# First attention of a fused four-stage kernel: scores of two heads on two row halves of TensorE, P divided on GpSimd, transposes late in a step

## What is computed

```python
h = silu(x @ W1.T + b1) @ W2.T + b2
q, k, v = split(h @ Wg.T + bg)              # 16 heads of 64
dots = einsum('bhid,bhjd->bhij', q, k) / 8
dots = where(j >= i + 64, -inf, dots)       # banded from above
attn = softmax(dots)
out  = einsum('bhij,bhjd->bhid', attn, v) @ Wo.T + bo
```

## Time and profile before

| | |
|---|---|
| median of 3 runs | 1743.43 us |
| span of the profiled execution | 1814.1 us |
| TensorE busy | 1434.0 us, 79% of the span |
| VectorE busy | 1064.9 us, 59% |
| ScalarE busy | 973.5 us, 54% |
| GpSimd busy | 448.9 us, 25% |
| first attention | about 34 to 770 us of the span |

### The profile page before, as it was taken

How to read it: one execution, slowest core, us unless ns; L and a number is a source line. 1 busy time by engine, 2 the same in 40 slices (tenths; PEclk the granted TensorE clock), 3 DMA queues, 4 the chain that set the end, 5 groups by cost and what they waited for, 6 DMA issues and landing times.

```text
span 1814.1 us, 32941 instructions
## 1 busy us (share of the span) xinstructions
PE 1434.0 (79%) x8094; PEld 974.1 (54%) x8094; DVE 1064.9 (59%) x3974; ACT 973.5 (54%) x2664; POOL 448.9 (25%) x495
## 2 busy tenths in 40 slices
PE   7999999999999999818999999125676667567581
PEld 4666665666665656416788888112344344335351
DVE  2677777777777777636443343025466556656555
ACT  6777777777777777414455555002344334334454
POOL 1012111222222212125100000665434433441003
PEclk9999999999999999859999999656788778878896
DMA  9000000000000000022122222144334333332301
GB/s 342 1 10 12 12 12 12 12 12 12 12 12 12 10 10 12 11 81 64 59 67 69 64 69 66 38 63 57 49 54 51 50 41 56 49 49 42 41 2 46
DMA packets 76443, 78.90 MB, mean 43 GB/s; under 512 B 10769, under 2 KB 69650, under 8 KB 75954
## 3 DMA queue, kind: packets, MB, share of 16 engines
q1 hardware_dynamic: 55378, 49.77, 13.9%
q0 software_dynamic: 8192, 16.79, 3.3%
q10 hardware_dynamic: 12816, 11.67, 1.9%
HBM read 47.92 MB, written 29.49 MB: 43 GB/s over the span
## 4 chain that ended last, share of the span: by engine, by line
PE 26%; DMA 11%; SPq 6%; issue 4%; DVE 3%; another core or an unknown queue 2%; ACT 1%; DVEq 1%; POOL 1%; POOLq 0%; ACTq 0%
PE psum L766 7%; PE psum L774 7%; DMA qst<-mrow 5%; SPq L425 3%; PE psum L810 3%; DMA wall<-mrow 3%; PE psum L799 2%; DMA qkd<-parts 2%; SPq L439 1%; PE psum L873 1%; PE psum L748 1%; PE psum L832 1%; PE psum L780 1%; POOL yk L543 1%
## 5 line engine op out<-in xcount | busy, mean ns | idle before, releaser
L947 ACT ACTIVATE P<-shifted,least 128x192 f32<-128x192 f32 (+1 forms) x512 | 240.9, 471 | 179.5 <-DVE least L1111 164.9
L1311 DVE TENSOR_REDUCE mx<-psum 128x2 f32<-128x512 f32 x256 | 165.6, 686 | 172.2 <-PE psum L873 128.3
L1010 ACT ACTIVATE wall<-psum 128x1024 f32<-128x1024 f32 x128 | 131.1, 1024 | 215.9 <-PE psum L799 153.2
L659 PE MATMUL psum<-kT,qT 128*128 128x384 f32 (+1 forms) x512 | 214.7, 542 | 0.0
L492 POOL DMA_INDIRECT xs<-x1c,pos x128 | 125.1, 978 | 335.2 <-DVE pos L1182 298.5
L1111 DVE CUSTOM_DVE_ANT_0 shifted<-psum,band 128x192 f32<-128x192 f32 (+1 forms) x512 | 170.6, 383 | 48.7 <-PE psum L659 32.9
L993 ACT ACTIVATE hid<-psum,wA 128x256 f32<-128x256 f32 x320 | 133.1, 471 | 66.3 <-PE psum L766 65.4
L766 PE MATMUL psum<-xgT,wA 128*128 128x256 f32 x640 | 157.5, 390 | 11.1 <-DVE xgT L1250 11.1
L674 PE MATMUL psum<-ident,P 128*128 128x128 f32 x1024 | 138.4, 278 | 18.7 <-DVE P L1104 18.6
L774 PE MATMUL psum<-hid,wB 128*128 128x256 f32 x640 | 151.4, 379 | 0.4 <-ACT yTe L997 0.4
L1104 DVE TENSOR_SCALAR P<-P,rinv 128x192 f32<-128x192 f32 (+1 forms) x512 | 145.1, 345 | 9.9
(11 more groups left out here) (244 smaller groups left out, 2649.6 us busy)
## 6 DMA issues: line engine op xcount, KB each, us to landing
xg<-xs SPq DMA_DIRECT2D x80, 128.0 KB, 2.0
ys<-yrow ACTq DMA_DIRECT2D x80, 128.0 KB, 1.7
wall<-in_wall SPq DMA_DIRECT2D x1, 8232.0 KB, 35.6
qkd<-parts SPq DMA_DIRECT2D x16, 384.0 KB
qst<-qkd SPq DMA_DIRECT2D x66, 64.0 KB
kst<-qkd SPq DMA_DIRECT2D x66, 64.0 KB
wall<-qkd SPq DMA_DIRECT2D x60, 64.0 KB
hT<-in_xT SPq DMA_DIRECT2D x4, 512.0 KB, 5.9
```

The costliest lines, as they stand in the source:

```text
L659: mm(bk[:, 0:2 * w].rearrange("q (h j) -> q h j", h=2), qT[:, p, it * 128:(it + 1) * 128], kT[:, p, :, 0:w], start=True, stop=True).then_i ...
L947: last = sc.activation(P[:, par, it, h, 0:w], shifted[:, par, it, h, 0:w], ACT.Exp, scale=-1.0, bias=least[:, par, n:n + 1], accum_out=row ...
L1010: sc.activation(pc[:, p % 4, :, :, :].rearrange("q h j n -> q (h j n)"), ST, ACT.Exp, scale=SCALE1).then_inc(s["exps1"], 1)
L1311: v.tensor_reduce(out=mx[:, :, h], in_=SB[(par + 1 + h) % 3].rearrange("q (i n) -> q i n", i=TT), axis=mybir.AxisListType.X, op=ALU.max).t ...
```

## The change

1. **Scores.** `kT` loses its zero padding (128 x 8 x 256 in place of 128 x 8 x 2 x 256). Each head's scores are a matmul of 64 rows of its own: first head on rows 0 to 63 into S0, second on rows 64 to 127 into S1. Four matmuls of 192 or 256 columns stand in place of two of 384 and 512. They wait for all four mask passes of the pair before. k leaves PSUM in one ScalarE instruction for both heads.
2. **P divided on GpSimd**, in the same step as its exponentials, behind that step's indirect DMAs. VectorE makes the reciprocals in two halves, head by head; ScalarE's exponentials go head by head.
3. **Transposes** of pair p-1 go from before P times V to the end of the step. VectorE copies both PTA and PTB, in the step after, as its first work; ScalarE copies neither.
4. At p = 6 the V projection goes behind the transposes. The output projection goes ahead of V's projection in the other steps. `hot` is one instruction in place of eight. The memset of the padding goes.

```diff
-        kT = sb("kT", [128, PAIRS, 2, N], c=a)
+        kT = sb("kT", [128, PAIRS, N], c=a)
...
# GpSimd, behind the DMAs of the step
+                    if is_pair(b, p, 0):
+                        par = p % 2
+                        for h in range(2):
+                            need_alone(pool, "rinv_ready", 2 * pair(b, p) + (h + 1))
+                            for it in range(TT):
+                                n = 2 * h + it
+                                x = P[:, par, it, h, 0:(N - WINDOW if it == 0 else N)]
+                                g.tensor_scalar(x, x, rinv[:, par, n:n + 1], None, ALU.mult).then_inc(s["pn_ready"], 1)
...
# TensorE
-                        for it, bk in ((0, S0), (1, S1)):
+                        need(pe, "shifted_ready", 4 * pair(b, p))
+                        for it in range(TT):
                             w = N - WINDOW if it == 0 else N
-                            need(pe, "shifted_ready", 4 * pair(b, p) - 2 * (1 - it) ...)
-                            mm(bk[:, 0:2 * w]..., qT[:, p, it * 128:(it + 1) * 128],
-                               kT[:, p, :, 0:w], start=True, stop=True).then_inc(s["scores"], 1)
+                            c0 = 0 if it == 0 else N - WINDOW
+                            for h, bk in ((0, S0), (1, S1)):
+                                last = mm(bk[:, c0:c0 + w], qT[64 * h:64 * h + 64, p, it * 128:(it + 1) * 128],
+                                          kT[64 * h:64 * h + 64, p, 0:w], start=True, stop=True)
+                                if it == TT - 1:
+                                    last.then_inc(s["scores"], 1)
# order behind qk and after_attention: PV, output projection, V projection, transposes, logits, V at p = 6
# (before: transposes, PV, V projection, output projection, logits)
...
# ScalarE
-                for h in range(2):
-                    sc.activation(kT[64 * h:64 * h + 64, r, h, :], J[64 * h:64 * h + 64, N:2 * N], ...)
+                sc.activation(kT[:, r, :], J[:, N:2 * N], ACT.Identity, bias=cols[:, 3 + PAIRS + r:4 + PAIRS + r]).then_inc(s["k_ev"], 1)
...
-                        sc.activation(PT[:, par1, 1, WINDOW:2 * N], PTB[:, WINDOW:2 * N], ACT.Copy).then_inc(s["ptB_ev"], 1)
...
# VectorE, first in a step
-                        need(dve, "exps", pair(b, p))
-                        v.reciprocal(rinv[:, par1, :], rowsum[:, par1, :])
-                        v.drain()
-                        ... four v.tensor_scalar(x, x, rinv[:, par1, n:n + 1], None, ALU.mult)
+                        need(dve, "pv_mm", pair(b, p, -3))
+                        for h, bk, ev in ((0, PTA, "ptA_ev"), (1, PTB, "ptB_ev")):
+                            need(dve, "pt_mm", 2 * pair(b, p, -2) + (h + 1))
+                            v.tensor_copy(PT[:, par, h, WINDOW:2 * N], bk[:, WINDOW:2 * N]).then_inc(s[ev], 1)
# VectorE, behind the mask passes of pair p
+                        for h in range(2):
+                            need(dve, "exps", 2 * pair(b, p) + (h + 1))
+                            v.reciprocal(rinv[:, par, 2 * h:2 * h + 2], rowsum[:, par, 2 * h:2 * h + 2]).then_inc(s["rinv_ready"], 1)
...
-                        for it in range(TT):
-                            for k in range(TOPK):
-                                v.tensor_scalar(hot[:, it, k, :], iota_e[:, :], topif[:, it, k:k + 1], None, ALU.is_equal)
+                        v.tensor_tensor(hot[:, :, :, :], iota_e ... to_broadcast([128, TT, TOPK, E]), topif ... to_broadcast(...), ALU.is_equal)
```

More of the change, by code:

```diff
@@ L706, in body @@
                         mm(Y[:, 0:N], wo[:, r, :], OT[:, par1, :], start=(r == 0), stop=(r == 7)).then_inc(s["wo_mm"], 1)
+                    if p == 0 and has(b, 0) and has(b, -1):
+                        need(pe, "pos_ready", b - 1)
+                        vproj(4 * b + 1, 0, 1)
+                    if p in (1, 2) and is_batch(b, 0):
+                        vproj(4 * b + (1 + p), 1, p - 1)
+                    if is_pair(b, p, -1):
+                        for h, bk, ev in ((0, PTA, "ptA_ev"), (1, PTB, "ptB_ev")):
+                            need(pe, "pn_ready", 4 * pair(b, p) - 2 * (1 - h))
+                            need(pe, ev, pair(b, p, -1))
+                            for jt in range(TT):
+                                for it in range(TT):
+                                    c0 = (N if jt == 0 else 0) + it * 128
+                                    last = nc.tensor.transpose(bk[:, c0:c0 + 128], P[:, par1, it, h, jt * 128:(jt + 1) * 128], ident[:, :])
+                            last.then_inc(s["pt_mm"], 1)
                     if p == 5 and is_batch(b, -1):
@@ L711, in body @@
                         last.then_inc(s["m_l"], 1)
+                    if p == 6 and is_batch(b, 1):
+                        need(pe, "hv_ready", b + 2)
+                        need(pe, "top_ready", b)
+                        vproj(4 * b + 4, 0, 0)
             def after_attention(b, p):
@@ L1094, in body @@
                     par, par1 = p % 2, (p - 1) % 2
-                    if is_pair(b, p, -1):
-                        need(dve, "exps", pair(b, p))
-                        v.reciprocal(rinv[:, par1, :], rowsum[:, par1, :])
-                        v.drain()
-                        for h in range(2):
+                    if is_pair(b, p, -2):
+                        need(dve, "pv_mm", pair(b, p, -3))
+                        for h, bk, ev in ((0, PTA, "ptA_ev"), (1, PTB, "ptB_ev")):
+                            need(dve, "pt_mm", 2 * pair(b, p, -2) + (h + 1))
+                            v.tensor_copy(PT[:, par, h, WINDOW:2 * N], bk[:, WINDOW:2 * N]).then_inc(s[ev], 1)
+                    if is_pair(b, p, 0):
+                        for h, bk in ((0, S0), (1, S1)):
+                            need_alone(dve, "scores", 2 * pair(b, p) + (h + 1))
                             for it in range(TT):
@@ L1156, in body @@
                         v.drain()
[L1157 to L1159 removed]
+                        v.tensor_tensor(hot[:, :, :, :], iota_e[:, :].rearrange("q (i k e) -> q i k e", i=1, k=1).to_broadcast([128, TT, TOPK, E]),
+                                        topif[:, :, 0:TOPK].rearrange("q i (k e) -> q i k e", e=1).to_broadcast([128, TT, TOPK, E]), ALU.is_equal)
                         v.drain()
```

58 lines of the change are left out of this document (11 added, 47 removed).

## The result

The changed kernel takes 1763.33 us (median of 5 runs, 1753.16 to 1767.2) against 1749.72 for the kernel before on the same chip: ratio 1.0088, 95% interval 1.0058 to 1.0119. By that ratio it is slower by some 15 us (the medians lie 13.6 apart), where 38.8 us less were forecast. Its profiled execution took 1753.16 us with a span of 1751.4.

What follows compares the result with a forecast made beforehand. TensorE was taken to bound the first attention: 2.4 us less in each of 15 batches (36) plus 2.8 in the first made -38.8, from 1743.4 to 1705 us; range for 8 in 10: 1670 to 1742.

Steps and rivals of the forecast that it cites:

- the price of the divide: GpSimd, four divides a step: 0.45 us each, ends 0.40 and 0.75, taken from a copy's 0.40.
- Hidden at either end of the range: GpSimd's divides in p = 0 to 3 stay behind TensorE's work, deciding only above 0.84 us each.
- the forecast batch of 44.0: First attention: TensorE's work of 39.8 us plus waits of 4.2, in place of 46.4 a batch.
- GpSimd becomes the bound: Rival, steps 0 to 3: above 0.84 us a divide GpSimd binds; at 1.2 us, 1800 in all; chance 0.09.
- The slack: GpSimd's divides begin about 2.7 us into a step, transposes want them 3.5 into the next: 3 us spare.
- two engines share SBUF: Argument for the rival that GpSimd binds: VectorE and GpSimd share SBUF; no size given.
- Waits: TensorE's standstills at p = 0, 5 and 7, late VectorE copies and x1T: 4.2 us a batch against 3.8 before.
- The other 3.8 us are waits: Kernel before, first attention: 42.6 us of TensorE's 46.40 us batch are work, the remaining 3.8 waits.
- the excursion into the divided array: TensorE's scores: entering and leaving row halves costs 0.40 us, leaving a saving of 0.35 a step.
- free excursion: Rival, scores: drain and loads of one half lie under the other; 72 us less, 1671; chance 0.12.
- bare loads: Rival, scores: weight loads unhidden in half mode, 0.31 us a step; some 5 us gained, 1738; chance 0.07.
- halves in turn: Rival, scores: row halves take turns, losing 0.40 us a step; 1788, slower; chance 0.08.

Runs made afterwards that it cites:

- g_cheap: The changed kernel with each GpSimd divide cut to the first 64 columns, part of the computation left out: 1728.88 us, ratio 0.9916 to the kernel before.
- h_fill: The changed kernel with four filler matmuls of 256 columns on TensorE in the wait at p = 0: ratio 1.0086 to the kernel before.
- c_actcopy: The changed kernel with PTB copied by ScalarE again, first in its step, and PTA by VectorE: ratio 0.9844 to the kernel before.
- e_copyfirst: The changed kernel with both PT copies of p = 0 moved to the end of p = 7, ahead of `pos`: 1817.2 us, ratio 1.0036, slower machine.
- o2_cheap47: The changed kernel with only the divides of p = 4 to 7 cut to 64 columns, part of the computation left out: ratio 0.9951.
- q2_best: The changed kernel with all divides on VectorE, PTB copied by ScalarE, p = 0's PTA copy ahead of `pos`, x1T ahead of q and k: 1694.58 us.
- n_dve: The changed kernel with PTB copied by ScalarE and all four divides on VectorE, none on GpSimd: 1724.23 us, ratio 0.9891.

## Why the prediction was wrong, by its own steps

**The step that failed** is the price of the divide: "a scalar per partition streams one, so I take 0.45, ends 0.40 and 0.75", and with it "Hidden at either end of the range. It decides once a divide costs over (...) = 0.84 us". The nearest row by number of inputs was a copy; the divide is 1.9 times as dear and above even the bound from the two-input row. `g_cheap` tests it: with divides of 0.445 us the same program has the forecast batch of 44.0 in three of four batches and 45.7 in the fourth, 44.4 on the mean, against 46.65: 2.25 x 15 = 34 us. Measured are 1728.88 against 1761.23, 32 us (two sets of runs, whose kernels before differ by 1 us). The 34 us hold three things that this run does not part: GpSimd's queue, VectorE's small instructions, which the prediction did not charge at all, and a clock that falls in a quarter of the batches and not in two thirds. And the price alone would not have saved the forecast: `g_cheap` is 17 us faster than the kernel before, not 38.8; the rest is the base, below. The rival "GpSimd becomes the bound" was there, with its place and threshold, and had 9 in 100; the value came to 0.845 against the 0.84 from which it "decides".

**The slack was counted to the wrong reader.** The threshold asked when the transposes would wait for P, and by it 0.845 would have cost nothing. The reader that matters is the power behind the 16 divides, and x1c behind it. The prediction named it ("Behind a late divide ... stand the next step's DMAs, the copy for V at p = 3 and the power at p = 4, which VectorE wants late in its step") and took it for harmless. It has no slack in the batches in which the clock holds, nor in `h_fill`, `c_actcopy` and `e_copyfirst`, because `pos`, at which the chain begins, is itself made from x1c. In the two of three batches with the clock fallen it has 0.9 us, and there the divides cost only what they take from VectorE.

**A term put at nothing.** VectorE's instructions were priced as in the kernel before. With divides in flight several are slower. `o2_cheap47`, which leaves GpSimd's piece of the chain as long as it was, gains 1.4 us a batch with the clock held and 0.7 with it fallen. The rival's "two engines share SBUF" had no price.

**Waits.** Forecast 1.4 at p = 0, 1.4 at p = 5, 1.2 at p = 7, 0.2 for others, in those places. Measured in the batch from 392.16, over the work of each step: p = 0 3.7 (2.0 of waiting and 1.7 of clock), p = 4 0.4, p = 5 1.45, p = 7 1.5. The places are right. At p = 5 the wait is 2.65 in the batches in which the clock holds. The late copies at p = 0 were seen, that they would cost the clock was not.

**The base.** "The other 3.8 us are waits" was true of the profiled execution; on the machine of the comparison they are 2.5. The prediction took the difference of 70.7 us between span and median over as a constant and said that no row says where it lies; 1.25 x 15 = 19 us of it were waits of the kernel before, which the change could not remove a second time. On the slower machine VectorE and ScalarE of the kernel before both stand still in steps 1 and 2 of a batch, for nothing the profile shows:

```profile
450.83 0.36 DVE L1111 CUSTOM_DVE_ANT_0 shifted<-psum,band 128x192 f32<-128x192 f32 x1 [1.69 <-remote]
451.23 0.46 ACT L947 ACTIVATE P<-shifted,least 128x192 f32<-128x192 f32 x1 [3.35 <-issue]
```

**The sum mended.** -38.8 + 19 (base) + 40 (waits, 2.65 x 15) = +20 us, against +22.8 at the end of the first attention. Of the whole time 15 to 17 are seen; the missing 6 to 8 are less than what the later stages differ by.

**What held.** Row halves run together; the excursion into the divided array costs 0.40, so the saving is 0.35 a step. Weight loads in the half mode are hidden, and the rivals of free excursion, bare loads and halves in turn all fall with the plain step of 4.43. ScalarE bought nothing by being relieved. x1T at p = 5 was late as described, and to move it ahead of q and k is one of the two moves that make `q2_best`.

**Open:** why the kernel before stands still on one machine alone; what the row halves alone, and the changed kernel, do on the other machine; what each of the two moves in `q2_best` is worth alone.

## What to carry to other kernels

Price an operation that the trace lacks by its own kind on that engine, and if there is no such row let the range reach well past the nearest one: here the spare time of a "free" engine was lost over a factor of 1.9. Ask for each queue not only who reads the moved work but who reads the small instruction behind it, and follow that reader round the loop: a chain that closes on itself once a batch has no slack, and TensorE's waits name only its last link. Look at several batches: here two paths lie 0.6 to 0.9 us apart, and which one is longer changes with the clock. A wait that disappears without a gain (`e_copyfirst`, `h_fill`) is the sign of such a chain; make the suspected link cheap and try the same edit again.

## What the runs showed of the hardware

**GpSimd's price has a slope.** In-place multiplication by a scalar per partition, float32: 0.445 us for 64 columns, 0.77 for 192, 0.93 for 256, some 2.5 ns a column. Its copy of 128 x 256 takes 0.40. The Trainium skill, GPSIMD Engine Reference, 4.1 (Engine selection), calls elementwise work with one input "roughly line-rate" against VectorE; for this form the runs disagree, 0.93 to 0.35.

**Divides on GpSimd slow some small instructions of VectorE.** Groups view, 112 to 700 us, of the kernel before, then after:

```profile
L1151 DVE TENSOR_SCALAR x1c<-res,mv,rstd 128x128 f32<-128x128 f32 x26 | 7.8, 344 | 2.9 <-issue 2.9
L85 DVE TENSOR_SCALAR veps<-mv 128x2 f32<-128x2 f32 x13 | 2.1, 161 | 0.0
L1168 DVE TENSOR_TENSOR rank<-rank,first_row 128x32 f32<-128x32 f32 x13 | 2.5, 192 | 1.0
L1130 DVE COPY PT<-psum 128x448 f32<-128x448 f32 x104 | 64.5, 621 | 7.9 <-PE psum L674 4.1
```

```profile
L1152 DVE TENSOR_SCALAR x1c<-res,mv,rstd 128x128 f32<-128x128 f32 x24 | 11.2, 599 | 2.8 <-issue 2.8
L85 DVE TENSOR_SCALAR veps<-mv 128x2 f32<-128x2 f32 x13 | 5.5, 422 | 0.0
L1168 DVE TENSOR_TENSOR rank<-rank,first_row 128x32 f32<-128x32 f32 x13 | 4.7, 361 | 1.0
L1104 DVE COPY PT<-psum 128x448 f32<-128x448 f32 x202 | 116.1, 616 | 4.5 <-issue 3.9 <-PE psum L712 0.6
```

Each of the three small ones takes 0.17 to 0.26 us more on the mean, whatever its size. So does `hot` (490 ns after, 292 in `g_cheap`), and L90, L92 and L94 between power and x1c take 0.12 to 0.16 more. veps stands ahead of the power, which waits for GpSimd's queue, so it costs nothing in the batches in which the clock holds. By their means the others make two x1c 0.51, L90 to L94 0.43, hot 0.20, rank 0.17, and topif, gate_all and posf_all 0.36: 1.7 us a batch, about the 1.6 that `o2_cheap47` gains in these pieces. Not slowed are the instructions that read PSUM, as the PT copy, and on SBUF the reciprocals (165 ns), reductions (286 and 369), statistics (286) and junk (L1174, 211), although divides run beside them too. In `g_cheap` (354, 160 and 193 ns) the small ones are back at the old price though shorter divides run beside x1c and rank; in `n_dve` (344 and 161 for the first two) no divides do. The Trainium skill, GPSIMD Engine Reference, 1 (Specifications), has the two engines share their SBUF interfaces, with contention for VectorE instructions "in a 2-port perf mode or with two SBUF inputs". The trace agrees in part: rank and hot, with two SBUF inputs, are slowed, but junk, with two as well, is not. Whether x1c and veps, with one tensor input, run in such a mode no run here shows.

**TensorE's clock** fell to its 1.2 GHz level after a standstill of 2.0 us in two batches of three, and held after the same standstill in the third. Four matmuls of 256 columns in that gap kept it up in every batch of `h_fill`.
